# Six groups of expert rows taken ahead of the plan, experts ordered by the picks of eight sequences

## The reference, cut to what matters

```python
x = x + conv(groupnorm(x))                      # 16 modes of an rfft, mixed, irfft
t = tokens(x)                                   # 4096 tokens = 16 sequences x 256, D = 256
t = t + attention(layernorm(t))                 # causal, one head, per sequence
h = layernorm(t)
topk_w, topk_idx = top_k(softmax(h @ router_w), 2)   # 8 experts
topk_w = topk_w / sum(topk_w)
for e in range(8):                              # w_fc[e] 256x1024, w_proj[e] 1024x256
    t = t + combine[:, e] * (gelu(h @ w_fc[e]) @ w_proj[e])
```

## Time and profile before

| | us |
|---|---|
| median of 3 runs (lowest, highest) | 686.19 (685.14, 688.24) |
| the profiled execution | 685.08 |
| its span, first to last instruction | 682.7 |
| PE busy in the span | 615.7 (90%) |
| DVE, POOL, ACT busy | 490.1, 404.6, 397.0 |

### The profile page before, as it was taken

How to read it: one execution, slowest core, us unless ns; L and a number is a source line. 1 busy time by engine, 2 the same in 40 slices (tenths; PEclk the granted TensorE clock), 3 DMA queues, 4 the chain that set the end, 5 groups by cost and what they waited for, 6 DMA issues and landing times. The chain is left out here.

```text
span 682.7 us, 15315 instructions
## 1 busy us (share of the span) xinstructions
PE 615.7 (90%) x4664; PEld 587.4 (86%) x4664; DVE 490.1 (72%) x1162; ACT 397.0 (58%) x694; POOL 404.6 (59%) x298
## 2 busy tenths in 40 slices
PE   2796999999820999999999999999999999999993
PEld 2685888888720999999999999999999999999993
DVE  7663668788777687786768778676877868766661
ACT  3704666776524465656666565666656566656661
POOL 5101121667877567676676667667666766777773
PEclk9996999999965899999999999999999999999997
DMA  8906741232338446523131322313132232312111
GB/s 345 308 2 246 262 162 39 82 110 105 136 110 220 97 142 180 149 57 47 31 63 31 57 37 46 48 31 63 31 56 38 46 48 32 56 24 41 32 25 16
DMA packets 37588, 62.35 MB, mean 91 GB/s; under 512 B 3696, under 2 KB 32944, under 8 KB 36400
## 3 DMA queue, kind: packets, MB, share of 16 engines
q0 software_dynamic: 13296, 18.00, 14.8%
q1 hardware_dynamic: 14816, 34.56, 14.5%
q10 hardware_dynamic: 9440, 9.36, 5.5%
HBM read 37.02 MB, written 24.89 MB: 91 GB/s over the span
## 5 line engine op out<-in xcount | busy, mean ns | idle before, releaser
L625 POOL TENSOR_TENSOR pj_lo<-w_ffn,pj_hi 128x1024 fp32r<-128x1024 f32 x78 | 189.0, 2429 | 101.5 <-ACT pj_hi L685 96.8
L1368 DVE TENSOR_TENSOR fc_lo<-w_ffn,fc_hi 128x1024 fp32r<-128x1024 f32 x78 | 113.4, 1487 | 79.1 <-ACT fc_hi L685 79.1
L614 POOL DMA_INDIRECT out<-y,add_id x71 | 112.7, 1587 | 42.5 <-issue 41.5
L685 ACT ACTIVATE pj_hi<-w_ffn 128x1024 fp32r x78 | 82.6, 1060 | 89.7 <-PE psO L1693 77.0
L685 ACT ACTIVATE fc_hi<-w_ffn 128x1024 fp32r x78 | 79.0, 1053 | 36.5 <-issue 35.9
L1693 PE MATMUL psP<-pj_hi,h_hi 128*128 128x256 f32 x312 | 92.2, 295 | 2.7 <-DVE h_lo L1368 2.7
L1693 PE MATMUL psP<-pj_hi,h_lo 128*128 128x256 f32 x312 | 88.5, 284 | 0.0
L1693 PE MATMUL psP<-pj_lo,h_hi 128*128 128x256 f32 x312 | 88.3, 283 | 0.0
L582 POOL DMA_INDIRECT slots<-rows,slot x64 | 64.1, 1001 | 18.3 <-issue 16.5
L572 POOL TENSOR_TENSOR roots<-ve,power 128x6 f32<-128x6 f32 (+2 forms) x20 | 23.0, 1152 | 86.6 <-DVE ve L1045 85.6
L1693 PE MATMUL psO<-pj_lo,h_hi 128*128 128x256 f32 x256 | 72.6, 283 | 0.0
(11 more groups left out here) (302 smaller groups left out, 1592.0 us busy)
## 6 DMA issues: line engine op xcount, KB each, us to landing
w_ffn<-in_w_ffn SPq DMA_DIRECT2D x8, 2048.0 KB, 7.8
xg<-slots ACTq DMA_DIRECT2D x31, 265.0 KB, 2.9
xc<-in_x_ch SPq DMA_DIRECT2D x4, 1024.0 KB, 8.5
out<-x SPq DMA_DIRECT2D x16, 256.0 KB, 2.2
x<-in_x_tok SPq DMA_DIRECT2D x1, 3072.0 KB, 24.6
slots<-fill SPq DMA_DIRECT2D x9, 265.0 KB, 5.9
out<-y,add_id POOLq DMA_INDIRECT x71, 3.9
w_in<-in_w_in SPq DMA_DIRECT2D x1, 1024.0 KB, 13.5
```

Source lines behind the costliest of these rows:

```text
L614: nc.gpsimd.indirect_dma_start(out_d, bass.IndirectOffsetOnAxis(ap=add_id[:, s:s + 1], axis=0), y[:, s, :], None, compute_op=ALU.add).then ...
L625: nc.gpsimd.tensor_tensor(pj_lo[:, 4 * a:4 * a + 4, :], w_ffn[:, bass.ds(e, 1), (2 + a) * DFF:(3 + a) * DFF].rearrange("p a (c d) -> p (a ...
L685: nc.scalar.activation(out, src, ACT.Copy, **kw).then_inc(done, 1)
L1368: v.tensor_tensor(out, whole, upper.bitcast(F32), ALU.subtract).then_inc(done, 1)
```

## The change: what it does

After batch 1 (eight sequences) the picks of each expert so far are summed on PE (`count_known`). In slot 12 DVE sorts the experts by that sum (`order_experts`), and in slot 13 it makes the table for six whole groups from the first five experts of that order (`first_counts`, `first_rows`). The weights are loaded in that order: three of them from slot 12 on, two after the attention, three when all rows are scattered; none is loaded before the attention any more. Group 0's rows are fetched in slot 14, its upper and lower parts are made in slots 14 and 15, and its `up` starts between the matmuls of slot 16. The last batch's routing (12 scatters with 10 of earlier batches), the plan of the other 26 whole groups and the plan of the half groups are cut up and put into groups 0 to 4, which have an order of their own (`relieved`). The wait for all scattered rows now stands before the fetch of group 6. The number of groups, and PE's work in a group, stay.

```diff
-EARLY = 11
+KNOWN = 1
+EARLY = sum(BATCHES[KNOWN])
...
+RESIDENT = E - LATE
+AHEAD = 6
+assert (EARLY * SEQ * PICKS * RESIDENT // E - RESIDENT * (GS - 1) + GS - 1) // GS >= AHEAD
+REST = FULL - AHEAD
...
+        def weights_in(eng, n):
+
+            if n:
+                eng.wait_ge(ld_w, 16 * n)
+            e = eng.value_load(order[0:1, n:n + 1], min_val=0, max_val=E - 1)
+            eng.dma_start(w_ffn[:, (n + LATE) % E, :],
+                          w_ffn_d[bass.ds(e, 1)].rearrange("a p n -> p (a n)")).then_inc(ld_w, 16)
...
-            for e in range(E - LATE):
-                weights_in(sp, e)
-
-            with sp.Fori(0, B) as b:
+
+            def store(b, landed):
+
                 sp.wait_ge(x2_ready, b * 2 + 2)
                 sp.dma_start(out_d[bass.ds(b * SEQ, SEQ)].rearrange("(s p) d -> p s d", p=P),
-                             x[:, bass.ds(b * 2, 2), :]).then_inc(x2_stored, 16)
+                             x[:, bass.ds(b * 2, 2), :]).then_inc(landed, 16)
+
+            with sp.Fori(0, STORED_FIRST) as b:
+                store(b, stored_first)
+            for b in range(STORED_FIRST, EARLY + 3):
+                store(b, stored_next)
+            sp.wait_ge(order_ready, 1)
+            weights_in(sp, 0)
+            for n, b in enumerate(range(EARLY + 3, EARLY + 5)):
+                store(b, stored_next)
+                weights_in(sp, n + 1)
+            for b in range(EARLY + 5, B - 1):
+                store(b, stored_next)
+
+
+            sp.wait_ge(meta_read, 2)
+            sp.wait_ge(xg_t_mm, 1)
+            load_group(sp, 1)
+            weights_in(sp, 3)
+            store(B - 1, stored_last)
+            weights_in(sp, 4)
...
                     root(k)
-                room = 1 if k == B else 5 if k < B else len(left)
+                if k == B + 1:
+                    return
+                room = 1 if k == B else 5
                 while left and room and k >= sum(BATCHES[batch_of(left[0][0])]) + 3:
                     scatter(*left.pop(0))
                     room -= 1
+
+            def scatter_some(n):
+                for _ in range(min(n, len(left))):
+                    scatter(*left.pop(0))
 
             pool.wait_ge(ld_route, 16 * 2)
...
-            add(0)
-            with pool.Fori(2, FULL) as g:
+                        pj_hi[:, 4 * a:4 * a + 4, :].bitcast(F32), ALU.subtract).then_inc(pj_lo_ready[a], 1)
+
+            pool_slot(B + 1)
+            scatter_some(2)
+            conv_rows_gone(pool)
+            pool.wait_ge(first_ready, 1)
+            for g in range(AHEAD):
+                proj_lower(g)
+                if g > 0:
+                    add(g - 1)
+                scatter_some(4)
+                assert g < AHEAD - 2 or not left
+
+            proj_lower(AHEAD)
...
+                if k == B - 2:
+                    act.wait_ge(first_ready, 1)
+                    act.wait_ge(scattered_early, SENT * EARLY)
+                    act.sem_inc(act_passed, 1)
+                    load_group(act, 0)
+                    act.wait_ge(spec_lower, B // 2)
+                    fc_upper(0, 0, range(0, 1))
+                if k == B - 1:
+                    fc_upper(0, 0, range(1, DH))
+                    x_upper(0)
+                if k == B:
+                    act.wait_ge(stored_first, 16 * (STORED_FIRST + 1))
+                    proj_upper(0, 0)
...
+                if relieved(g):
+                    proj_upper(g, 1)
+                    if g == 1:
+                        pick_ratio(len(BATCHES) - 1)
+                    gelu(g, 0)
+                    if g_on(g - 1):
+                        outputs(g - 1)
+                    if g == 0:
+                        normalise(B - 2, B + 1, 0, rows[:, 2 * B - 4:2 * B - 2, :], xn2_ready)
+                    gelu(g, 1)
+                    fc_upper(g + 1, 1 - par, range(0, 1))
+                    gelu(g, 2)
+                    fc_upper(g + 1, 1 - par, range(1, DH))
+                    gelu(g, 3)
+                    if g == 0:
+                        normalise(B - 1, B + 2, 0, rows[:, 2 * B - 2:2 * B, :], xn2_ready)
...
+                    if isinstance(g, int) and g + 2 == AHEAD:
+                        slots_there(act)
+                        act.wait_ge(idle_stored, 16)
...
                     weigh(j)
                 for j in batch_at(k - 2):
                     pick(j, 0)
                 for j in batch_at(k - 3):
                     pick(j, 1)
                     count_picks(j)
+                    if j == KNOWN:
+                        known_sum()
...
+                    x_lower(0)
 
             plan_steps = [0]
 
@@ -1272,48 +1437,69 @@
                 dve.wait_ge(plan_step, plan_steps[0])
 
             n_slots, n_groups, ends, ones, whole = (counts[:, n] for n in range(5))
-            was = tiles_in(len(BATCHES) - 1)
-            step(v.tensor_tensor(carry[:, :], before[:, 0:E * was].rearrange("p (e t) -> p e t", e=E)[:, :, was - 1],
-                                 picked[:, was - 1, :], ALU.add))
...
+            def tail_early(g):
+
+                if g == 0:
+                    pick(last, 0)
+
+                if g == 1:
+                    weigh(last)
+                if g == 4:
+                    half_groups()
+
+            def tail_ending(g):
+
+                if g == 0:
+                    pick(last, 1)
+                    gap_scale(last)
+                    count_picks(last)
+                    carry_out()
+                if g == 1:
+                    alone(counts_mm, 1)
+                    where_in(last)
+                    find_slots(last)
+                    counts_out()
+                if g == 2:
+                    plan_ends()
+                    plan_rows()
+                if g == 3:
+                    plan_weights()
+                    half_counts()
+
             def dve_group(g, par):
-                if is_half(g):
+                if relieved(g):
+                    hidden(g, 0)
+                    hidden(g, 1)
+                    e = expert_of(g + 1) if g + 1 < AHEAD else None
+                    if e is None:
+                        planned(dve, g + 1)
+                        e = expert_of(g + 1)
+                    fc_lower(g + 1, 1 - par, e, range(0, 1))
+                    slot_meta(g + 1)
+                    tail_early(g)
+                    if g == 0:
+                        alone(xn2_ready, 2 * B - 2)
+                    hidden(g, 2)
+                    hidden(g, 3)
+                    x_lower(g + 1)
+                    fc_lower(g + 1, 1 - par, e, range(1, DH))
+                    tail_ending(g)
...
+                if k == B:
+                    up(0, 0, range(0, 1))
                 if on(k - 1):
                     probs_t(k - 1)
+                if k == B:
+                    up(0, 0, range(1, 2))
...
+                if k == B - 1:
+                    x_transposes(0)
```

584 lines of the change are left out of this document (355 added, 229 removed).

## The result

| | before | after |
|---|---|---|
| median of 4 runs each (lowest, highest), us | 685.66 (684.97, 688.24) | 708.57 (706.23, 710.3) |
| ratio, 95% interval | | 1.0329 [1.0304, 1.0354] |
| the profiled execution, and its span | 685.08, 682.7 | 709.35, 707.6 |
| first matmul of group 6 | 297.5 | 320.8 |
| from there to the end of the span | 385.2 | 386.8 |

The account below looks back on a forecast made before the run. PE bounds steady groups, DVE the first ones; the change can fill a hole of some 34 us. Group 0 comes 13.4 us ahead, given back in five groups: group 6 at 299.1 against 297.3, so 688.0 us, range 675 to 697.

Parts of the forecast that it names:

- slots 12 and 13: DVE late: Ordering and table instructions on DVE make batch 2's `gap` 7.3 us late; PE gets p_t 7.0 us late.
- groups 0 to 4: From hidden(0, 0) to hidden(5, 0) DVE sets the pace: steps of 17.7, 13.5, 15.0, 16.2 and 15.7 us.
- The missing weight loads ... free no one: Before the attention, dropping loads gains nothing, as PE's slots have no pause; the early loads land by 203, in time.
- Rival 2: Slower: group 6's fetch waits on ACT for scatters and fills; at 291 it costs 5 us more, plus 2 clock: 695; chance 0.17.
- All by 0.20 us a small instruction: DVE's work in the first groups was priced at 0.20 us per small instruction and 0.42 per wide one.
- Both signs of being wrong: The forecast is wrong if slots 14 and 15 keep 7.6 us, or groups 1 to 5 take under 13 us each.
- The wait of ACT in group 4: ACT stands before group 6's fetch, awaiting scatters and fills: 2.8 us in group 4's step, range 0 to 8.
- Rival 1: Faster: DVE does not set the first groups' pace; group 6 starts at 286.8, 10.5 us earlier, median 677.5; chance 0.32.
- Rival 3: The change doesn't do what it says: fewer than six groups are known early; chance 0.01.
- The two table loads: In group 1 ACT loads tables around `ratio`, 1.28 us each without drain; the skill page would add 2.8 us.
- The difference at this point is the difference of the times: From group 6's start both kernels have the same groups, so the difference there is the whole difference.
- upper bound for the pace: Groups 0 to 4 were to take between PE's 11.92 and 16.5 us each: 0 to 23 us for five groups, 15 taken.

Follow-up runs that it names:

- e7: e3 with the first groups' tables one sequence later and group 0's fetch and its upper and lower parts moved from slot 14 into slot 15; 693.51 us.
- e3: The changed kernel with group 0's fetch ahead of the third weight load and its row transposes behind the last sequence's scores; 705.37 us.
- e1: The changed kernel with POOL writing zeros instead of subtracting in groups 0 to 5, those lower parts of the down projection left out; 694.76 us.
- e4: The changed kernel with the eight fills issued when the counts are there, not at the end of the plan; 705.41 us.
- e2: The changed kernel with the down projection's lower parts of groups 0 to 5 made by DVE instead of POOL, nothing left out; 700.58 us.
- e16: The changed kernel run again as it is; 706.92 us, ratio 1.030 to the kernel before.

## Why the prediction was wrong, step by step

| step | forecast | measured |
|---|---|---|
| start of the attention | as before | 2.6 us later at the keys of sequence 14 (173.43 for 170.80) |
| slots 12 and 13: DVE late | 7.3 us | `ratio` 182.08 for 172.96, less the 2.6 above: 6.5 |
| last sequence's keys | 178.47 + 9.0 = 187.5 | 189.51, 2.6 of it from the start of the attention |
| wait for the fetch of group 0 | none | 3.90 us |
| hidden(0, 0) | 211.2 | 217.9 |
| groups 0 to 4 | 78.1 | 92.1 |
| hidden(5, 0) to group 6 | 9.8 | 10.8 |
| group 6 against before | +1.8 | +23.3 to 23.5 |
| from group 6 on | 0 | +1.4 to 1.6 |

**What bounds it, and the slots: right.** The chains were priced well: `first_counts` and `first_rows` run from 175.18 to 180.64, 5.5 us for 5.3. PE waits 3.68 and 2.39 us, 6.1 for the 7.0 forecast, and the clock takes its share. One releaser was missed: the 3.68 us were for `where`, which stands behind the tables too, and not for p_t. Bringing the tables one slot later (e7) starts the last sequence 7.9 us earlier than in e3, of the 9.0 that this step had charged, and 4.8 of them reach group 0.

**"The missing weight loads ... free no one": wrong by omission.** The loads that were not missing but moved were held against DMA only as to when they land, not as to what they do to a small fetch beside them. The fetch of group 0 took 10.4 us; e3, which also moves its transposes, gets 6 us back. Rival 2 had a late fetch, but the other one.

**Start of the attention: not forecast, not explained.** The first keys start 0.8 us later, and the granted clock comes back to 1.00 after 69 us instead of between 66 and 67. The changed kernels lie 0.8 to 2.9 us late at sequence 14, so it differs between executions; what makes it so is open.

**Groups 0 to 4: the step that failed.** "All by 0.20 us a small instruction" is true of the earlier trace rows, where POOL did nothing but roots and transfers. In groups 0 to 4 they stand beside two subtractions of 2.4 us. There DVE is held 22.5 us. With POOL's subtractions out (e1) the five steps take 77.4 us for 78.1, so the duration was taken from a stretch with another neighbour. That the sum fits so well is partly luck: by steps e1 has 15.0, 13.6, 16.2, 15.8 and 16.8 us for 17.7, 13.5, 15.0, 16.2 and 15.7, group 0 priced too high and groups 2 and 4 too low, and POOL's writes still hold DVE in places. The rows had a sign of it, read as plain cost: in a steady group two fc_lo take 3.14 us, where two of 1.22 take 2.4. Of the 21.7 us missed at group 6 (320.8 for 299.1), 14.0 come in these five groups, 6.7 are there at hidden(0, 0), mostly the start of the attention and the fetch, and 1.0 behind hidden(5, 0). Both signs of being wrong that the prediction named (slots of 7.6 us, groups under 13) were for a faster kernel.

**The wait of ACT in group 4, rival 2: real, mis-sized.** The wait was 15.0 us and the fills decided it, and it cost some 1.6 us (e4), where the forecast had 2.8 and rival 2 had 7. Rival 1, for which DVE would not set the pace, falls: DVE's time is paid about one for one (e1, e2). Its 677.5 us is also a slip: 10.5 us is the distance from 297.3, so the median to take it from was 686.2, which gives 675.7. Rival 3 falls: six groups ran ahead.

**The two table loads: the row was right.** Loads of 1.28 us stand on both sides of `ratio`. The second follows it at once (238.06), and the gelu starts at 239.35, so no drain shows; nor does one at the first gelu (load at 214.41, gelu at 215.70). Behind the load ahead of `ratio` (235.03) ACT waited 1.52 us for `gap`, so a drain could hide there. The 2.8 us by the Trainium skill (ScalarE: Activation LUTs, What ACT_TABLE_LOAD costs) would have been too much.

**From group 6 on.** A group takes 11.78 us from one first matmul to the next, for 11.95 (851 matmuls in 100 us for 839), 4 us in all, and this is not explained. Against it stand 6 us at the end of this execution, where the last half group's fc_lo was held (e16's profile, without the hold, has 5 us less behind group 6). "The difference at this point is the difference of the times" holds within 1.6 us by luck.

**The range.** It was built from PE, DVE and POOL each by itself. Its upper bound for the pace, 16.5 us a group, was passed (18.4 us a group in the mean), because the one row with the two engines side by side had been read as plain cost.

## What to carry to other kernels

The duration of a small instruction belongs to the neighbour it was measured beside: before work is moved, ask which instruction of the other engine will run there, and read the longest and not only the mean duration of such pairs. On an engine that already bounds a stretch, every moved instruction costs its full time, and so does every hold. When one wait is removed from an engine that works in order, look first at what stands behind it there: here each of four rearrangements gave its gain back on POOL or in the transfers.
